# Two wide attentions of a decoder as one pipeline over units of four heads, every product as three fp32r products

## The reference

```python
# layer 1, windowed: 16 heads of 128, 4 key/value heads; a token sees itself and the 127 before it
q, k, v = x @ Wq, x @ Wk, x @ Wv
x = layernorm(x + softmax(mask(q @ k.T / 128)) @ v @ Wo)
# layer 2, cross: 16 heads of 128, 8 key/value heads; keys and values from ctx (8, 256, 256), masked
q, k, v = x @ Wq, ctx @ Wk, ctx @ Wv
x = layernorm(x + softmax(mask(q @ k.T / sqrt(128))) @ v @ Wo)
# then: experts, two attentions of 32 heads of 16 (narrow), a feed-forward part with Hadamard transforms
```

## Time and profile before

| | |
|---|---|
| median of 3 runs | 3812.82 us (3812.54 to 3815.93) |
| profiled execution, its own span | 3845.9 us |
| instructions | 53,358 |
| TensorE matmul busy | 3445.7 us, 90% |
| TensorE weight load busy | 2411.1 us, 63% |
| VectorE busy | 1766.5 us, 46% |
| ScalarE busy | 1243.2 us, 32% |
| GpSimd busy | 287.5 us, 7% |
| mean granted clock | 0.942 of 2.4 GHz |
| HBM read, written | 138.30 MB, 50.47 MB |

### The profile page before, as it was taken

The page is one execution under the profiler, slowest core; times in us unless marked ns, Lnnn a source line. Parts: engine busy times, 40 slices in busy tenths (PEclk is TensorE's granted clock), DMA queues, the critical chain, the costliest instruction groups (busy, mean ns, idle before and its releaser), DMA issues. The chain is left out here.

```text
span 3845.9 us, 53358 instructions
## 1 busy us (share of the span) xinstructions
PE 3445.7 (90%) x18745; PEld 2411.1 (63%) x18746; DVE 1766.5 (46%) x5115; ACT 1243.2 (32%) x2730; POOL 287.5 (7%) x317
## 2 busy tenths in 40 slices
PE   7999999989999999976993999998888866999996
PEld 6666777767777777754442565555555534777774
DVE  4433333344444344432116455556666636444345
ACT  1223333333333333323111343434454544122121
POOL 2222000003000000004122000000000000000000
PEclk8999999999999999986996899999999978999998
DMA  6511111114111111113333000000000011000001
GB/s 244 187 39 44 44 44 44 44 60 145 47 46 46 41 41 42 41 63 142 104 125 99 2 3 2 8 21 18 5 8 5 2 45 23 12 22 11 22 11 44
DMA packets 83093, 191.63 MB, mean 50 GB/s; under 512 B 23424, under 2 KB 27520, under 8 KB 81864
## 3 DMA queue, kind: packets, MB, share of 16 engines
q0 software_dynamic: 32912, 100.03, 8.5%
q1 hardware_dynamic: 50048, 89.82, 6.8%
HBM read 138.30 MB, written 50.47 MB: 49 GB/s over the span
## 5 line engine op out<-in xcount | busy, mean ns | idle before, releaser
L1805 DVE TENSOR_REDUCE mx_n<-bank 128x6 f32<-128x768 f32 (+1 forms) x256 | 279.8, 1093 | 179.5 <-PE bank L1581 109.1
L1713 ACT ACTIVATE probsT_n<-bank 128x768 f32<-128x768 f32 (+1 forms) x256 | 235.7, 921 | 296.4 <-PE bank L1600 159.9
L447 PE MATMUL bank<-wo_x,work_x 128*128 128x512 f32 x512 | 227.2, 594 | 5.1 <-ACT work_x L479 3.8
L447 PE MATMUL bank<-wo_s,work_s 128*128 128x512 f32 x512 | 227.3, 594 | 5.0 <-ACT work_s L479 3.8
L479 ACT ACTIVATE work_s<-bank 128x512 f32<-128x512 f32 (+1 forms) x224 | 104.2, 465 | 352.9 <-PE bank L436 171.2
L479 ACT ACTIVATE work_x<-bank 128x256 f32<-128x256 f32 (+1 forms) x240 | 109.6, 460 | 322.8 <-PE bank L436 188.6
L584 DVE CUSTOM_DVE_ANT_0 work_x<-bank,work_x 128x256 f32<-128x256 f32 x256 | 97.8, 419 | 220.6 <-issue 220.6
L1575 PE MATMUL bank<-kT_n,qT_n 48*128 48x256 f32 (+1 forms) x1024 | 125.5, 324 | 76.0 <-DVE mx_n L1805 74.9
L525 ACT ACTIVATE work_x<-work_x 128x256 f32<-128x256 f32 x256 | 128.3, 503 | 196.0 <-DVE work_x L589 196.0
L584 DVE CUSTOM_DVE_ANT_0 work_s<-bank,const 128x128 f32<-128x128 f32 (+1 forms) x256 | 80.8, 353 | 217.3 <-issue 217.3
L525 ACT ACTIVATE work_s<-work_s 128x128 f32<-128x128 f32 (+1 forms) x256 | 114.5, 448 | 182.0 <-DVE work_s L589 182.0
(11 more groups left out here) (376 smaller groups left out, 7120.3 us busy)
## 6 DMA issues: line engine op xcount, KB each, us to landing
wq_lo_s<-wq_lo_s POOLq DMA_DIRECT2D x64, 512.0 KB, 3.6
wq_lo_x<-wq_lo_x POOLq DMA_DIRECT2D x64, 512.0 KB, 3.5
expert_rows<-table_zero SPq DMA_DIRECT2D x20, 512.0 KB, 14.7
work_m<-expert_rows SPq DMA_DIRECT2D x40, 256.0 KB, 2.7
expert_products<-work_m POOLq DMA_DIRECT2D x40, 256.0 KB, 2.7
expert_table<-table_zero SPq DMA_DIRECT2D x16, 512.0 KB, 14.0
weights_m<-expert_table SPq DMA_DIRECT2D x4, 2048.0 KB, 9.7
ug_rows<-in_L_ffn_W_gate SPq DMA_DIRECT2D x9, 512.0 KB, 3.7
```

The lines of the kernel that those rows point to most:

```text
L447: last = pe.matmul(out[t][:, :], oT[:, h, t * P:(t + 1) * P], wo[:, h, :], start=(h == 0), stop=(h == H - 1), skip_group_check=True)
L1713: act.activation(probsT[:, turn_ % SLOT_PAIRS, :, 0:cols], scoreT[:, :, 0:cols], ACT.Exp, scale=SCALE)\
L1805: dve.tensor_reduce(to.rearrange("p t h -> p h t"), seen, AX.X, ALU.max).then_inc(s["scores_read"], 1)
```

## The change

Both wide attentions become one block, and the loops change places: a unit is 4 query heads of one stage (8 units a stage, 16 in all); it comes twice over items, an item being a pair of sequences with these four heads. An item has 8 steps, one for each head and sequence. All 256 steps stand in one instruction stream without loops over sequences, in which step t has the scores of step t-3, half a query product for two sequences (512 columns), the transposes of step t-5, a side product (transposes of x or context, keys, values, by the table `side`), the values of step t-6 and a part of the output of step t-11.

Every product is made of three fp32r products; ScalarE writes the rounded part and VectorE the remainder (queries, keys, values, transposed probabilities, heads, x, context). Weights are loaded in pieces of 128 x 512 into four staging buffers, and GpSimd splits each into `hi` and `lo` in SBUF, ten pieces a unit; nothing of them goes to HBM. The output product of four heads is added to x in place (`add_output`), so x holds the running sum over units; the norm of two sequences comes in five parts inside the steps after their last unit. The mask is applied with a negative scale and a minimum, which removes the negation. The masks are loaded at the start of the one block, and context rows are masked by GpSimd. The clearing of the experts' rows and the table additions are spread over the pieces.

```diff
-def ln_vector(dve, chip, out_banks, batch, s, it):
...
+HEADS_OF_UNIT, STAGED, ROUNDS_OF_PROBS = 4, 4, 3
+STAGE_UNITS = 8
+UNITS = 2 * STAGE_UNITS
+ITEMS_WIDE = 2 * UNITS
+WIDE_STEPS = 8 * ITEMS_WIDE
...
+        wo = lambda u: [("wo", u, h) for h in range(4)]
+        wq = lambda u: [("wq", u, h) for h in range(4)]
+        self.first = [("wk", 0, 0), ("wv", 0, 0)] + wq(0)
+        self.pieces = list(self.first)
+        for u in range(UNITS):
+            n = u + 1
+            if n < STAGE_UNITS:
+                self.pieces += [("wk", n, 0)] + wo(u) + [("wv", n, 0)] + wq(n)
+            elif n < UNITS:
+                self.pieces += wo(u) + [("wk", n, 0)] + wq(n)[0:3] + [("wv", n, 0)] + wq(n)[3:]
...
+        kind, u, h = self.pieces[n]
+        if n >= STAGED:
+            sp.wait_ge(*self.split_at[n - STAGED])
...
+        pool.tensor_copy(hi, whole).then_inc(self.rounded, 1)
+        pool.wait_ge(self.rounded, n + 1)
+        pool.tensor_tensor(lo, whole, hi.bitcast(FP32), ALU.subtract).then_inc(self.split[kind], 1)
...
+    for i in range(ITEMS_WIDE):
+        base = 8 * (i - 1)
+        if i % 8 < 2:
+            if cross(i):
+                for k, at in enumerate((0, 1)):
+                    put(base + at, ("c", i, k))
+            for k, at in enumerate((4, 5, 6, 7) if cross(i) else (0, 1, 4, 5)):
+                put(base + at, ("x", i, k))
+        for at, what in ((((-1, ("k", i, 0)), (3, ("k", i, 1)), (2, ("v", i, 0)), (6, ("v", i, 1))) if cross(i) else
+                          ((-5, ("k", i, 0)), (-1, ("k", i, 1)), (-2, ("v", i, 0)), (2, ("v", i, 1))))):
+            put(8 * i + at, what)
...
+            sp.dma_start(mask8, mask_dram.rearrange("b s -> (b s)").partition_broadcast(P)).then_inc(s["mask_loaded"], 16)
+            with nc.allow_non_contiguous_dma(reason="2048 mask bytes onto the partitions"):
+                sp.dma_start(maskcol8, mask_dram.rearrange("b (t p) -> p (b t)", p=P)).then_inc(s["mask_loaded"], 16)
...
+            for n in range(first_pieces, len(w.pieces)):
+                kind, u, h = w.pieces[n]
+                if u >= 1:
+                    i = 2 * u - 1
+                    if kind == "wk":
+                        pool.wait_ge(s["side_ready"], nth["k", i, 1])
+                    elif kind == "wv":
+                        pool.wait_ge(s["side_ready"], nth["v", i, 1])
+                    elif kind == "wq":
+                        pool.wait_ge(s["q_ready"], 4 * i + h + 1)
+                    else:
+                        pool.wait_ge(s["out_half"], 8 * i + (6 if h < 2 else 8))
+                w.divide(pool, n)
+                if kind == "wq" and 1 <= u <= 4:
+                    at = 2 * (4 * (u - 1) + h)
+                    table.add_sets(pool, range(at, at + 2))
...
+            def thrice(a, b, chunks):
+                hi_a, lo_a = a
+                hi_b, lo_b = b
+                return [(f(cc), g(cc)) for f, g in ((hi_a, hi_b), (hi_a, lo_b), (lo_a, hi_b)) for cc in range(chunks)]
...
+                elif kind == "k":
+                    pe.wait_ge(w.split["wk"], unit_of(i) + 1)
+                    if cross(i):
+                        weight = [lambda cc, a=a: a[:, cc * 2 * P + k * P:cc * 2 * P + (k + 1) * P] for a in (w.hi["wk"], w.lo["wk"])]
+                        moving = [lambda cc, a=a: a[:, par, cc, :] for a in (ctx_hi, ctx_lo)]
+                        last = products(b[:, :], thrice(weight, moving, CC))
+                    else:
+                        weight = [lambda cc, a=a: a[:, cc * P:(cc + 1) * P] for a in (w.hi["wk"], w.lo["wk"])]
+                        moving = [lambda cc, a=a: a[:, par, cc, k * SEQ:(k + 1) * SEQ] for a in (x_hi, x_lo)]
+                        last = products(b[:, 0:SEQ], thrice(weight, moving, DC))
+                else:
+                    pe.wait_ge(w.split["wv"], unit_of(i) + 1)
+                    source, chunks = ((ctx_hi, ctx_lo), CC) if cross(i) else ((x_hi, x_lo), DC)
+                    width, at = (2 * P, k * P) if cross(i) else (P, 0)
+                    moving = [lambda cc, a=a: a[:, cc * width + at:cc * width + at + P] for a in (w.hi["wv"], w.lo["wv"])]
+                    for m, tile in enumerate(range(4) if cross(i) else (2 * k, 2 * k + 1)):
+                        weight = [lambda cc, a=a: a[:, par, cc, tile * P:(tile + 1) * P] for a in source]
+                        last = products(b[:, m * P:(m + 1) * P], thrice(weight, moving, chunks))
+                last.then_inc(s["side_ready"], 1)
...
+                weight = [lambda cc, a=a: a[:, h, cc, :] for a in (w.hi["wq"], w.lo["wq"])]
+                moving = [lambda cc, a=a: a[:, i % 2, cc, :] for a in (x_hi, x_lo)]
+                all_ = thrice(weight, moving, DC)
+                for n in range(6 * part, 6 * part + 6):
+                    last = pe.matmul(pair_bank(j)[:, :], *all_[n], start=(n == 0), stop=(n == 11), skip_group_check=True)
+                if part:
+                    last.then_inc(s["q_ready"], 1)
...
+                for t in range(TILES):
+                    keys = SEQ if cross(i) or t else P
+                    at = slice(q * SEQ + t * P, q * SEQ + (t + 1) * P)
+                    kk = slice(q * SEQ, q * SEQ + keys)
+                    hi, lo = q_hi[:, n // 2 % 2, at], q_lo[:, n // 2 % 2, at]
+                    last = products(score[n % 2][:, t * SEQ:t * SEQ + keys],
+                                    [(hi, k_hi[:, slot, kk]), (hi, k_lo[:, slot, kk]), (lo, k_hi[:, slot, kk])])
+                last.then_inc(s["scores_ready"], 1)
...
+                for k in range(TILES):
+                    q0 = 0 if cross(i) else k * P
+                    at = slice(k * SEQ, (k + 1) * SEQ - q0)
+                    vh, vl = v_hi[:, slot, q, k, :], v_lo[:, slot, q, k, :]
+                    ph, pl = p_hi[:, n % 2, at], p_lo[:, n % 2, at]
+                    for a, b in ((vh, ph), (vh, pl), (vl, ph)):
+                        last = pe.matmul(obank[:, col + q0:col + SEQ], a, b, start=(m == 0), stop=(m == 5), skip_group_check=True)
+                        m += 1
+                last.then_inc(s["heads_ready"], 1)
...
+                for h in (2 * part, 2 * part + 1):
+                    slot = oT_slot(i, h, q)
+                    hi, lo = o_hi[:, slot, t * P:(t + 1) * P], o_lo[:, slot, t * P:(t + 1) * P]
+                    for a, b in ((hi, w.hi["wo"]), (hi, w.lo["wo"]), (lo, w.hi["wo"])):
+                        first = h == 0 and a is hi and b is w.hi["wo"]
+                        last = pe.matmul(out[t][:, :], a, b[:, h, :], start=first, stop=(h == 3 and a is lo), skip_group_check=True)
+                last.then_inc(s["out_half"], 1)
...
+            for t in range(FIRST, END):
+                if live(t - 3):
+                    scores(t - 3)
+                if live(t):
+                    query(t)
+                if live(t - 5):
+                    turn(t - 5)
+                for what in side.get(t, ()):
+                    side_use(t, what)
+                if live(t - 6):
+                    values(t - 6)
+                if live(t - 11):
+                    output(t - 11)
...
+            norm_at = {8 * i + at: (i, part) for i in range(ITEMS_WIDE) if last_unit(i)
+                       for part, at in enumerate((16, 20, 21, 22, 23))}
+            dve.wait_ge(s["mask_loaded"], 32)
+            dve.tensor_copy(maskcol[:, :], maskcol8).then_inc(s["maskcol_ready"], 1)
+            for t in range(FIRST, WIDE_STEPS + 16):
+                m = t - 12
+                if 0 <= m < WIDE_STEPS and m // 2 % 2:
+                    add_output(m)
+                if live(t - 3):
+                    mask(t - 3)
+                if t % 2 == 0 and live(t - 2):
+                    j = t // 2 - 1
+                    dve.wait_ge(s["q_hi"], j + 1)
+                    remainder(q_lo[:, j % 2, :], pair_bank(j)[:, :], q_hi[:, j % 2, :]).then_inc(s["q_lo"], 1)
+                if live(t - 4):
+                    normalise(t - 4)
+                if live(t - 5):
+                    n = t - 5
+                    cols = 2 * SEQ if cross(n // 8) else SEQ + P
+                    dve.wait_ge(s["probsT_hi"], n + 1)
+                    remainder(p_lo[:, n % 2, 0:cols], trans[:, 0:cols], p_hi[:, n % 2, 0:cols]).then_inc(s["probsT_lo"], 1)
+                for what in side.get(t, ()):
+                    dve.wait_ge(s["side_hi"], nth[what])
+                    remainder(side_target(what, 1), side_source(t, what), side_target(what, 0)).then_inc(s["side_lo"], 1)
+                if live(t - 6):
+                    n = t - 6
+                    slot = oT_slot(*step_of(n))
+                    dve.wait_ge(s["heads_hi"], n + 1)
+                    remainder(o_lo[:, slot, :], obank[:, n % 2 * SEQ:(n % 2 + 1) * SEQ], o_hi[:, slot, :]).then_inc(s["heads_lo"], 1)
+                if t in norm_at:
+                    norm_part(*norm_at[t])
...
+            for n in range(len(weights.first)):
```

(18 more changed lines are left out.)

675 lines of the change are left out of this document (297 added, 378 removed).

## The result

The changed kernel takes 3712.78 us (median of four runs, 3709.48 to 3726.03), the kernel before on the same chip 3813.41 us (four runs). The ratio is 0.9727, 95% interval 0.97 to 0.9754: 2.7% faster. Timed once more later, against another nine runs of before, it came to 0.9709 (0.9693 to 0.9725). The forecast was faster by 3.6%, 3677 us; the measured time lies in its range and in the narrower one of the likeliest case, 36 us above the forecast itself. The profile is of the slowest of the four runs (3726.03 us, a span of 3724.4 between first and last instruction).

A forecast was written before the change was run, and what follows sets the result against it. TensorE's instruction stream was taken as the bound: 54 us start, 1,455 of products and 56 of overhead end the attentions at 1,565 instead of 1,702 us; scaled, that gave 3,677 us, own range 3,635 to 3,730.

The forecast's parts named there:

- the likeliest case: Whole kernel: the forecast of 3,677 us itself, given 67% and its own range of 3,635 to 3,730 us.
- products without transposes of x and context: Both attentions: TensorE's sum per head and sequence, 5.63 us windowed and 5.75 cross, 1,455 us together with these transposes.
- transposes, norms, GpSimd, side products: Wide pipeline: normalising 7 us, GpSimd delaying VectorE 10, side products waiting 2; transposes were counted in TensorE's 1,455 us.
- fill, low clock, end, borders: Wide part's edges: fill 23 us, low clock over part of the fill 4, the end 8, block borders 2.
- TensorE bounds the steady part: Between heads of both attentions, TensorE's instruction stream is the bound, so the change is costed as matmuls times distance.
- Prices: TensorE's fp32r products: 0.227 us at 512 columns, 0.12 at 256, and 0.120 taken at 128, between 0.110 and 0.225.
- The rival of four passes: Narrow products: 2,304 at 0.225 instead of 0.12 us add 242 us, giving 3,919 us; chance 10%.
- the one of faster weights: Narrow products: weights reload in 0.081 us, 90 us less, giving 3,587 us; chance 5%.
- VectorE held by GpSimd: Wide part: GpSimd's delays of VectorE reach TensorE, 5 us a unit cost 80 us, giving 3,757 us; chance 13%.
- Weights late, longest chain: Wide pipeline: late weights or the longest chain, one step's wait a unit, 91 us, giving 3,768 us; chance 5%.
- Normalising inside the pipeline ... 1 us each for seven, 7 us: Wide pipeline: normalising 8 times, each putting 2.9 us into one VectorE step with slack in neighbouring steps; 7 us.
- Fill and end, 37 us: Start and end of the wide part: fill 23 us, low clock 4, end 8, with block borders 2.

The follow-up runs named there:

- the base: The changed kernel without further edits, from which the follow-up experiments start; 3712.78 us, ratio 0.9727 to the kernel before, 0.9709 when timed again.

## Why the prediction was right, and 36 us short

By its own steps, for the stretch of the two attentions (forecast 54 to 1565 us, measured 53 to 1597). The steady rate holds no transposes of x and context, so they are subtracted from the forecast's products here (128 x 0.055 + 128 x 0.085 = 18 us) and counted with the norms:

| term | forecast, us | measured, us |
|---|---|---|
| products without transposes of x and context | 1455 - 18 = 1437 | 16 x 44.1 + 16 x 45.25 = 1430 |
| transposes, norms, GpSimd, side products | 18 + 7 + 10 + 2 = 37 | 64.5 |
| fill, low clock, end, borders | 23 + 4 + 8 + 2 = 37 | 1544 - 1430 - 64.5 = 50 |
| sum | 1511 | 1544 |

By the forecast's own sum for the kernel before, products and transposes take 1533 us of its 1648; here they take 1430 and, at the forecast's price of transposes, 18. So of the 104 us won they brought 85 (78 forecast) and all the rest 19 (59 forecast): what is not matmuls was mis-sized, not TensorE's work.

- **TensorE bounds the steady part: right, shown.** The items follow the sum of TensorE's distances when products are taken off (42.75 and 41.29 us, each as worked out) and when they are added (46.78 against 46.98). VectorE is busy 58 and 66% of the halves (60 to 70% forecast).
- **Prices: right.** 512 columns 0.23, 256 columns 0.12. The unknown one, 128 columns, was taken as 0.12 between 0.110 and 0.225; it is 0.112, next to the lower end, and the clue was the row of eight columns. That the sum comes within 7 us is in part luck. Distances between starts in a steady item of each half, times sixteen: products of 512 columns stand 0.233 to 0.236 us apart on average, not 0.227 (some 24 us more), those of 256 cost 19 more than at 0.12, those of 128 some 30 less, and transposes 0.08 to 0.09 instead of 0.11 (some 22 less).
- **The rival of four passes, and the one of faster weights: false.** Both fall with 0.112. The Trainium skill (TensorE: Matmul & The Clock Gate, section Back-to-back issue gap) gives about 81 ns for a stream of weight loads and 128-column products; the trace does not agree for four-byte weights, 112 ns.
- **VectorE held by GpSimd: false as a bound**, some 1.5 us in waits and what clock falls with them, of the 10 taken; twice the subtractions cost nothing in any steady item, and 11 us at the norms. Its clue was misread: GpSimd's subtraction of the earlier trace rows ends at 101.29 (98.92 and 2.37 us), and the 1.91 us of the earlier trace rows begin at 101.46. Beside them GpSimd issues a DMA and makes its rounding copy (102.16, 1.05 us). What stood beside the subtraction is VectorE's L589 on two columns, 1.01 us instead of 0.17. The rows of the changed kernel above show the effect that was meant, 1.76 instead of 0.61 us.
- **Weights late, longest chain: false.** No wait of TensorE for a split weight appears between the first output product and the last item.
- **"Normalising inside the pipeline ... 1 us each for seven, 7 us": the step that was off most.** The forecast put the 2.9 us into one step of VectorE and counted on "slack in neighbouring steps". But the chain stands ahead of the query remainder, and TensorE needs that within the same step: the chain comes through nearly whole, as waits of 2.1 to 3.3 us, 16 us in all. And the forecast left out that the clock may fall behind such a wait. In the first profile of the base the clock is low seven times between the first output and the last item, 55 us together, which costs half of it, 27 us. Six falls come behind the norm's waits, and one behind a wait of 1.5 us for a side product. Spreading the chain took 30 us out of the pipeline; lengthening it put 20 in. The rest of the 64.5 us are the transposes, of which the forecast had 18 for the whole part (14 of them here), and the waits of one side product for the remainder of the one before it in the same bank; the forecast had 2 us for those, the wait rows show 6.3 and 4.5. Together that is 68 us, 4 more than measured.
- **Fill and end, 37 us: 13 too low, mostly the clock.** The wait for the mask was seen (6 us forecast, 5.8 from the first transposes to its arrival), and taking it away gives 5 us back. The fill took 28.3 us to the first query against 23. The low clock was taken at 4 us. It lasted to 87 us:

```profile
53.00:87.00 34.00, 21.35 (x80) 17.89 (x81) 4.80 (x9) 4.14 (x8) 0.00 (x0) 0.50 0.15 39
87.00:131.00 44.00, 41.05 (x290) 37.08 (x289) 24.35 (x85) 19.93 (x62) 13.71 (x15) 1.00 0.23 77
1535.00:1589.00 54.00, 48.95 (x284) 41.82 (x282) 36.76 (x110) 18.46 (x53) 0.00 (x0) 0.97 0.00 1
1589.00:1597.00 8.00, 0.00 (x0) 0.00 (x0) 5.82 (x22) 0.00 (x0) 0.00 (x0) 0.70 0.00 1
```

  TensorE's 21.35 busy us at 1.2 GHz are 10.7 us more than at 2.4, and 0.03 of 54 us are 1.6 at the end: 12 us against 4. TensorE is idle for 12.7 + 3.0 + 5.1 + 8.0 = 29 us in the four stretches, and 32 transposes of the first two items are 3.5. That is 45 of the 50 us; the missing 5 stand against the 4 too many above. Over all of 1544 us the account closes: 1430 of products, 18 of transposes, 56 of idle TensorE and 40 of clock.
- **The wide part misses by 33 us and the time by 36.** That the two agree is partly chance. The rest of the kernel was 16.5 us shorter in this profile than in that of before, and the forecast took it as equal; but the profiled execution also stands only 12 us above the median of its runs, where the forecast scaled by the 33 of before. The two nearly cancel.
- **Other signs.** Steps were forecast 5.6 to 5.8 us apart and are 5.51 and 5.66. GpSimd is busy 356 us in the wide part, not 330: a piece takes 0.61 + 1.29 = 1.9 us instead of 1.7. Two lists in the forecast don't add up to what stands beside them: the gain of 78 us leaves out the queries (0.08 us a step, 20 us) and puts what narrow products give back at 60 instead of 72, and VectorE's terms make 3.8 us a cross step, not 3.9 (measured: 509.8/128 = 4.0). The sums that the forecast uses are not touched.
